# Two-layer graph kernel on one core: ScalarE normalises all rows of layer one's first eight blocks, the link factors are turned inside layer one, and layer two's first loads go out beside layer one's last stores

## What is computed

```python
edge_index = jnp.stack([src, dst])
h = jnp.maximum(_layernorm(x, axis=-1), 0.0)
# layer one: h @ W_self.T + b_self + segment_sum(h[col] @ W_neigh.T + b_neigh, row) / clip(count, 1)
x = x + _L0_gnn_ref(h, edge_index, L0_gnn_W_self, L0_gnn_b_self, L0_gnn_W_neigh, L0_gnn_b_neigh)
h = jnp.maximum(_layernorm(x, axis=-1), 0.0)
# layer two: relu(segment_sum(h[src] * norm[:, None], dst)), norm = deg[src] ** -0.5 * deg[dst] ** -0.5
x = x + _L1_gnn_ref(h, edge_index)
```

## Time and profile before

| | |
|---|---|
| median of 3 runs | 1185.05 us (1183.37 to 1186.17) |
| profiled execution, its own time | 1182.12 us |
| span of the profiled execution | 1180.3 us |
| busy: PE, DVE, ACT, POOL | 90%, 90%, 92%, 73% of the span |
| first gather of layer one, first gather of its last block | 27.8 us, 673.6 us |
| first row of layer two on ScalarE | 737.7 us |

### The profile page before, as it was taken

One profiled execution on the slowest core, in us unless ns is written; L12 is line 12 of the kernel. 1 busy time (PEld: TensorE's weight loads), 2 busy tenths in 40 slices (PEclk: granted clock), 3 DMA queues, 4 the chain that ended last, 5 costly groups with the idle time before them and its releaser, 6 DMA issues.

```text
span 1180.3 us, 30320 instructions
## 1 busy us (share of the span) xinstructions
PE 1057.1 (90%) x9408; PEld 955.5 (81%) x9408; DVE 1057.1 (90%) x3040; ACT 1082.5 (92%) x2871; POOL 862.4 (73%) x1143
## 2 busy tenths in 40 slices
PE   1388999999999999999999993799999999999998
PEld 1377999999989988989889992688888888888886
DVE  7779989989989989989989853899999999999995
ACT  2378999999989999999999991999999999999997
POOL 4767777777777877777777714888888888888870
PEclk9689999999999999999999997555555555555555
DMA  6325666767666766776667526499999999999994
GB/s 209 120 71 166 209 197 207 222 190 215 190 202 200 197 214 188 208 198 204 208 194 216 186 98 235 133 297 293 291 282 288 288 282 292 281 285 289 288 288 168
DMA packets 82232, 259.39 MB, mean 220 GB/s; under 512 B 19987, under 2 KB 20357, under 8 KB 82117
## 3 DMA queue, kind: packets, MB, share of 16 engines
q1 hardware_dynamic: 58948, 210.86, 57.3%
q0 software_dynamic: 22400, 46.91, 13.7%
q10 hardware_dynamic: 768, 0.20, 0.1%
HBM read 152.93 MB, written 104.37 MB: 218 GB/s over the span
## 4 chain that ended last, share of the span: by engine, by line
ACT 56%; POOL 15%; issue 11%; DVE 7%; PE 7%; DMA 3%; POOLq 0%; ACTq 0%; DVEq 0%
ACT work L739 24%; ACT p_O L739 14%; POOL X L634 12%; ACT p_T L739 6%; ACT area L754 4%; ACT p_c L739 3%; ACT area L749 2%; DMA X<-in_x,IDX 2%; DVE ST L1333 2%; PE p_O L910 2%; ACT sd L717 2%; POOL work L596 1%; PE p_O L922 1%; POOL work L592 1%; DVE p_O L1376 1%
## 5 line engine op out<-in xcount | busy, mean ns | idle before, releaser
L739 ACT ACTIVATE work<-X,shift,scale 128x128 f32<-128x128 f32 x1372 | 564.7, 512 | 1.8 <-DVE shift L1367 1.8
L634 POOL DMA_INDIRECT X<-in_x,IDX x392 | 387.4, 988 | 127.4 <-issue 98.6
L1333 DVE BATCH_NORM_STATS2 ST<-X 128x6 f32<-128x256 f32 x1176 | 408.2, 415 | 26.7 <-DMA X<-in_x,IDX 24.9
L968 PE MATMUL p_O<-work 32*128 32x128 f32 x1984 | 307.0, 436 | 44.4 <-DVE work L1350 24.8
L634 POOL DMA_INDIRECT X<-x_table,IDX x294 | 286.3, 974 | 76.5 <-issue 61.7
L968 PEld LDWEIGHTS p_O<-work 32*128 32x128 f32 x1984 | 263.9, 323 | 87.8 <-ACT work L739 31.1
L910 PE MATMUL p_O<-wnT,area 128*128 128x128 f32 x1568 | 218.0, 283 | 0.0
L922 PEld LDWEIGHTS p_O<-wsT,area 128*128 128x128 f32 x1568 | 207.2, 193 | 7.6
L922 PE MATMUL p_O<-wsT,area 128*128 128x128 f32 x1568 | 207.8, 276 | 0.0
L739 ACT ACTIVATE p_O<-X,shift,scale 128x128 f32<-128x128 f32 x496 | 199.1, 442 | 0.6 <-DVE shift L1367 0.6
L910 PEld LDWEIGHTS p_O<-wnT,area 128*128 128x128 f32 x1568 | 193.0, 194 | 0.3 <-DVE area L1386 0.3
(11 more groups left out here) (173 smaller groups left out, 1191.9 us busy)
## 6 DMA issues: line engine op xcount, KB each, us to landing
x_table<-area SPq DMA_DIRECT2D x98, 528.0 KB
X<-x_table SPq DMA_DIRECT2D x98, 528.0 KB
X<-in_x SPq DMA_DIRECT2D x98, 512.0 KB, 4.6
out_x<-area SPq DMA_DIRECT2D x98, 512.0 KB, 6.9
X<-in_x,IDX POOLq DMA_INDIRECT x392
X<-x_table,IDX POOLq DMA_INDIRECT x294
moved<-held SPq DMA_DIRECT2D x32, 12.2 KB
es<-in_src SPq DMA_DIRECT2D x1, 488.5 KB, 3.5
```

The lines of the kernel that those rows point to most:

```text
L634: nc.gpsimd.indirect_dma_start(got(s)[:, k, 0:w], None, table, bass.IndirectOffsetOnAxis(ap=IDX[:, s, k:k + 1], axis=0)).then_inc(gathered ...
L739: last = nc.scalar.activation(o, row(l, s, r), ACT.Relu, bias=shift[:, s, r:r + 1], scale=scale[:, s, r:r + 1])
L968: last = nc.tensor.matmul(outs1[p][g][:, P * col:P * col + P], SEL[1][q, p, part_of, :], H[1][q, p, draw, :], start=False, stop=(half == 1 ...
L1333: last = V.bn_stats(ST[:, s, r:r + 2, :].rearrange("p r k -> p (r k)"), pair.rearrange("p r c -> p c r"))
```

## The change

- **Rows.** For blocks 0 to 7 (`FIRST = 8`) ScalarE normalises all 12 rows; GpSimd's `last_row` begins with block 8.
- **Index lots.** `LOT[0]` is 2 where it was 5: GpSimd stages row numbers for two blocks at a time (49 copies for layer one where it had 20).
- **Start.** SyncE's first six loads wait until window 0 has arrived. VectorE's two digit cuts ahead of `marks(0)` now stand behind `double(0)`; the bias is split by GpSimd and ScalarE ahead of the windows; the work on group 1 moves from steps -4 to 3 to steps -1 to 6, `BEGIN` for group 2 from step 3 to 7. `START_AHEAD` grows over 15 blocks where it was 10.
- **Link factors.** They are transposed, two pieces in a step, in steps 82 to 85, and ScalarE copies them there (`take_dis`); SyncE spreads them in steps 86 to 89, VectorE adds two of them in step 93.
- **Layer two's first loads.** SyncE issues one of the eight behind each of layer one's last eight stores.

```diff
-LOT = (5, 4)
+LOT = (2, 4)
-START_AHEAD = (1, 1, 1, 1, 2, 2, 2, 3, 3, 3)
+START_AHEAD = (1,) * 4 + (2,) * 5 + (3,) * 6
+STARTING = 7
+FIRST = 8
-    BEGIN = {2: 3, 3: 17, 4: 31, 5: 45, 6: 58}
+    BEGIN = {2: 7, 3: 20, 4: 33, 5: 46, 6: 59}
+    TURN_AT, PASS_AT, DIS_AT = 82, 86, 93
+    def rows_of(i):
+        return range(0, ROWS if i < FIRST else ROWS - 1)
+    def dis_groups(k):
+        return [g for g in range(TB) if TURN_AT + g // 2 == k]
...
                 store(l, turn, old)
+                early = old + RING[0] - NB
+                if l == 0 and 0 <= early and old % RING[0] < RING[1]:
+                    b = old % RING[0]
+                    sp.wait_ge(stored[0][b % HR[0]], 16 * (b // HR[0] + 1))
+                    load(1, 0, b)
+            sp.wait_ge(s_win[0], 16)
             for s in range(EARLY):
                 load(0, 0, s)
...
             for s in range(EARLY, RING[0]):
+                sp.wait_ge(st_ready[0], s - EARLY + 2)
                 load(0, 0, s)
...
+                if k == PASS_AT:
+                    sp.wait_ge(s_disl, TB // 2 + 1)
+                    if PASS_AT + n // 4 == k:
+                        sp.dma_start(moved[to, 2, slot_of(of), :], DISL[of, j, :]).then_inc(s_moved, 16)
...
             def last_row(turn, off):
                 i, s, _ = place(0, turn, off)
+                if i < FIRST:
+                    return
...
+            def take_dis(k):
+                act.wait_ge(s_disT, dis_groups(k)[-1] // 2 + 1)
+                for g in dis_groups(k):
+                    c = slice(GROUP_BLOCKS * g, GROUP_BLOCKS * g + GROUP_BLOCKS)
+                    for a in range(2):
+                        q = slice(SLOTS * a, SLOTS * a + SLOTS)
+                        last = nc.scalar.copy(DISL[q, :, c].rearrange("p j n -> p n j"), ...)
+                last.then_inc(s_disl, 1)
...
                 if joins is not None:
                     turn_codes(joins)
+                for g in dis_groups(off):
+                    pe.wait_ge(s_dis2, 1)
+                    last = nc.tensor.transpose(turned_dis(g), dis2[:, g, :, :].rearrange("p a b -> p (a b)"), ident[0:TP, 0:TP])
+                    if g == dis_groups(off)[-1]:
+                        last.then_inc(s_disT, 1)
...
+                if dis_groups(off):
+                    pe.wait_ge(s_disl, dis_groups(off)[-1] // 2 + 1)
...
-                if off == NB:
-                    pe.wait_ge(s_dis2, 1)
-                    pe.wait_ge(prod_used[1], NB - 2)
-                    pe.wait_ge(sdeg_ready, NB)
-                    for b in range(TB):
...
+                if k == DIS_AT:
+                    dve.wait_ge(s_moved, 16 * 3 * 4 * PAIRS)
+                    V.tensor_tensor(moved[:, 2, 2, :], moved[:, 2, 2, :], moved[:, 2, 3, :], ALU.add).then_inc(s_tab1, 1)
...
             def fast():
-                act.wait_ge(s_disl, 1)
-                for to, of, j in moves():
-                    act.dma_start(moved[to, 2, slot_of(of), :], DISL[of, j, :]).then_inc(s_moved, 16)
                 schedule(1, act, step1)
...
             def fast():
-                dve.wait_ge(s_moved, 16 * 3 * 4 * PAIRS)
-                V.tensor_tensor(moved[:, 2, 2, :], moved[:, 2, 2, :], moved[:, 2, 3, :], ALU.add).then_inc(s_tab1, 1)
                 schedule(1, dve, step1)
```

More of the change, by code:

```diff
@@ L147, in joins_at @@
     def joins_at(k):
[L149 to L157, removed]
+        return 1 if k == 5 else next((g for g in BEGIN if BEGIN[g] + 11 == k), None)
+    def dis_groups(k):
+        return [g for g in range(TB) if TURN_AT + g // 2 == k]
     def either(eng, fast, general):
@@ L367, in gnn @@
         s_bias = sem("bias_placed")
+        s_bsum = sem("bias_rests_ready")
         s_tab = sem("group_tables_ready")
@@ L495, in general @@
             def general():
+                for s in range(RING[1]):
+                    sp.wait_ge(x_loaded[s], 16 * (len(range(s, NB, RING[0])) + 1))
                 sp.wait_ge(g_clean, 1)
@@ L543, in window @@
                     bass.IndirectOffsetOnAxis(ap=ptr_i[:, b:b + 1], axis=1)).then_inc(s_win[b], 16)
+            pool.wait_ge(s_w, 64)
+            nc.gpsimd.tensor_tensor(bsum[0:1, 0, :], brow[0:1, 0, :], brow[0:1, 1, :], ALU.add).then_inc(s_bsum, 1)
+            for k in range(2):
+                pool.wait_ge(s_bpart, k + 1)
+                nc.gpsimd.tensor_tensor(bsum[0:1, (k + 1) % 2, :], bsum[0:1, k % 2, :], bpart[0:1, k, 0, :], ALU.subtract
+                                        ).then_inc(s_bsum, 1)
             pool.wait_ge(s_ptr, 1)
@@ L572, in may_gather @@
                 i, s, _ = place(l, turn, off)
+                if l == 0 and i == EARLY:
+                    pool.wait_ge(s_found, 2)
+                    pool.wait_ge(s_facts, 4)
+                    pool.wait_ge(s_digits, 2 * len(CUTS))
+                    pool.sem_inc(idx_seen[0], 1)
                 if not first(i, RING[l]):
@@ L706, in _ @@
             nc.scalar.copy(wnT[:, :], p_O[2][:, D:2 * D]).then_inc(s_wcopied, 1)
-            digit(0)
-            digit(1)
+            for k in range(3):
+                act.wait_ge(s_bsum, k + 1)
+                nc.scalar.copy(bpart[0:1, k, :, :], bsum[0:1, k % 2, :].rearrange("p (j d) -> p j d", j=1
+                                                                                  ).to_broadcast([1, GT, D])).then_inc(s_bpart, 1)
             take_codes(0)
-            for n in range(2, 2 * len(CUTS)):
+            for n in range(2 * len(CUTS)):
                 digit(n)
@@ L785, in step0 @@
                 if there(0, turn, off + 1):
-                    normalise(0, turn, off + 1, range(MID, ROWS - 1))
+                    normalise(0, turn, off + 1, rows_of(off + 1)[MID:])
             def step1(turn, off):
@@ L794, in _ @@
             schedule(0, act, step0)
-            act.wait_ge(s_disT, 1)
-            for o, i in table_parts(DISL, banks_dis):
-                last = nc.scalar.copy(o, i)
-            last.then_inc(s_disl, 1)
             def fast():
-                act.wait_ge(s_disl, 1)
-                for to, of, j in moves():
-                    act.dma_start(moved[to, 2, slot_of(of), :], DISL[of, j, :]).then_inc(s_moved, 16)
                 schedule(1, act, step1)
@@ L1485, in then @@
                     dve.wait_ge(g_ord, order[0] if order[1] is None else order[1] + order[0])
+                for s in range(EARLY, RING[1]):
+                    dve.wait_ge(x_loaded[s], 16 * (len(range(s, NB, RING[0])) + 1))
                 dve.wait_ge(g_ord, 1)
```

93 lines of the change are left out of this document (39 added, 54 removed).

## The result

The changed kernel took 1189.54 us (median of 5, 1188.35 to 1191.19) where the kernel before took 1183.68 us (median of 5, 1182.39 to 1186.17): ratio 1.0047, interval 1.0033 to 1.006. It is half a per cent slower; the forecast of 1178 us and its range of 1170 to 1183.5 were wrong. The profiled execution took 1189.54 us (span 1187.7; before 1182.12 and 1180.3).

What follows compares the result with a forecast made beforehand. POOL, at 6.68 us a block, was taken to bound the end of layer one. Its terms gave +9.5 us, then -2.6, +0.7 and -0.5: 7.1 us faster, 1185.05 to 1178 us, range 1170 to 1183.5.

Steps and rivals of the forecast that it cites:

- (e): Layer one on POOL: 29 more index copies at 0.22 us each cost 6.4 us, lower bound 3.
- (c): Early blocks on POOL: no more waiting for group 1's row numbers, gain 4.7 us, bound 0.
- (a): Start of layer one: POOL's first gather comes 2.9 us earlier, as loads no longer share window 0's way.
- (d): POOL around block 13: new waits for TensorE from doubled statistics at steps 6 and 11, cost 3 us, bounds 0 and 8.
- (b): First eight blocks: POOL is spared eight last rows at 1.41 us each, gain 11.3 us.
- (g): Last stores of layer one: layer two's early loads delay the last store, cost 0.5 us, bounds 0 and 1.9.
- (f): End of layer one: link factors add 5.9 us on ACT and PE, 3.3 hidden, so cost 2.6.
- PE's tail: Seam: the link factors' transposes leave TensorE's tail, gain about 0.7 us.
- the prediction's own sign of being wrong: Early layer one: POOL waiting for DVE or PE before block 14 would show the forecast wrong; no size given.
- Slower: Rival, chance 0.08: each of the 29 index copies costs POOL 1.0 us, total 15 us slower, 1200 us.
- Start not won: Rival, chance 0.20: TensorE's half clock slows the first blocks, block 6 at 105 or later; gain 0 to 4 us.
- Larger gain: Rival, chance 0.17: no new waits, half-price copies, factor copies hidden in ACT's slack; gain 11 to 16 us.

Runs made afterwards that it cites:

- exp. 6: Kernel before with index lots of two in layer one (29 more copies), nothing else: 1192.11 us, ratio 1.0067.
- exp. 8: exp. 2 with POOL doing the last row of every block again (FIRST = 0): 1188.04 us, ratio 1.0036.
- exp. 2: Changed kernel with STARTING = 11, early loads behind all stores and link factors back at the seam: 1176.99 us, ratio 0.9923.
- exp. 3: Changed kernel with STARTING = 11 and link factors back at the seam, early loads kept: 1177.25 us, ratio 0.9948.
- exp. 1: Changed kernel with STARTING = 11 in place of 7, nothing else: 1181.63 us, ratio 0.9958.
- experiment 7: exp. 2 with index lots of two for the first 30 blocks only, then five: 1169.7 us, ratio 0.9883; 1450.18 us on a slow chip.
- experiment 4: Changed kernel with only the link factors back at the seam, STARTING left at 7: 1188.16 us, ratio 1.0034.
- experiment 5: Changed kernel with only layer two's first loads behind all stores; slow chips only: 1492.52 us (1.0229) and 1471.68 us (1.0269).
- experiment 9: experiment 7 with ScalarE taking the twelfth row for 16 blocks (FIRST = 16); slow chip only: 1481.23 us, ratio 1.0335.

## Why the prediction was wrong

Seven kernels, from the one before to the changed one, form a chain in which neighbours differ by one edit, or, in its second link, by all edits of the start. The differences of their ratios, at 1184 us, price each link. Such a difference is uncertain by 2 to 3 us (the intervals are 0.3% wide), so the differences of the medians (the kernel before at 1183.97) and of the start of layer two in the traces stand beside it; the chain closes by construction. Negative is slower.

| link | from, to (ratio) | by ratios | by medians | by traces | forecast |
|---|---|---|---|---|---|
| 29 copies (e), part of (c) | before, exp. 6: 1, 1.0067 | -7.9 | -8.1 | -9.9 | -6.4 |
| start (a), (d), rest of (c) | exp. 6, 8: 1.0067, 1.0036 | +3.7 | +4.1 | +4.2 | +4.6 |
| eight last rows (b) | exp. 8, 2: 1.0036, 0.9923 | +13.4 | +11.1 | +11.6 | +11.3 |
| early loads (g) | exp. 2, 3: 0.9923, 0.9948 | -3.0 | -0.3 | -1.7 | -0.5 |
| factors (f) and PE's tail | exp. 3, 1: 0.9948, 0.9958 | -1.2 | -4.4 | -4.9 | -1.9 |
| `STARTING` 11 to 7 | exp. 1, changed: 0.9958, 1.0047 | -10.5 | -7.9 | -6.6 | not in the sum |

The forecasts of the first two rows put all of (c) into the second, though the short lots of the first already end POOL's wait for group 1. Only the sum of both rows is a fair comparison: -4.2 us by the ratios for a forecast of -1.8.

**The step that failed is (d), the new waits.** It took -3 with a bound of -8, for VectorE's doubled statistics at steps 6 and 11. POOL waited 13.64 us before the last rows of blocks 9 to 13, which is the prediction's own sign of being wrong (POOL waiting for PE before block 14). Some 3 us of these are of the size that (d) gave: with the old order 3.32 are left. The other ten have another reason, `STARTING = 7`, a line in the diff to which the sum gave no term. I had read POOL's order around the first `last_row` and never followed ACT's and VectorE's order in steps 7 to 11, where the change moves a root ahead of a spill. Without it (experiment 1) the kernel is faster than the one before, with it slower, and both are clear of noise. At 1181.63 us experiment 1 is in the range, 3.6 above the forecast; the rest lies within the sizes of (e), (f) and (g), none of which is measured sharply.

`STARTING = 7` makes no instruction longer and adds none. ACT takes its instructions in order, so a wait ahead of the spill is one for TensorE, VectorE and POOL. The Trainium skill ("PSUM — Partial Sum Buffer", section "Engine vs sequencer instructions") says that the queues of ScalarE, VectorE and GpSimd are strictly first in, first out. The trace agrees for ScalarE: in step 8 TensorE's transposes for `spill_h` were done at 105.76 (the row L900 above), 2.99 us before the root in front of it began at 108.75, and the spill started only behind the root.

**(a) Earlier first gather: right, and for the reason given.** 27.77 to 24.74, 3.03 us for 2.9. From issue to landing, window 0 took 6.26 us before and 3.22 after the change:

```profile
7.92 6.26 DMA win<-in_pairs,ptr_i
```

```profile
8.00 3.22 DMA win<-in_pairs,ptr_i
```

**(b) Eight last rows: right in kind and size.** POOL's path sets the end of layer one; 11.1 us at block 92 and 11.05 us in the medians.

**(c) Group 1: right.** POOL did not wait before block 8, whose `last_row` began at 91.40 (forecast 94), 19.3 us earlier than before. "Step 6 ends at 90 to 94" was right too: `decode(1)` at its end was done on VectorE at 92.05, 0.6 us before POOL's copy for block 14 began at 92.65, and ACT's last row of that step ended at 94.27. That the wait is gone is the lots' doing and not the start's (experiment 6).

**(e) Copies: kind right, their own price right, the effect at the end perhaps larger.** In the changed kernel:

```profile
470.27 0.45 POOL L624 TENSOR_SCALAR work<-X,scale,shift 128x128 f32<-128x128 f32 x1
470.91 0.54 POOL L628 TENSOR_SCALAR work<-work 128x128 f32<-128x128 f32 x1 [0.20 <-POOL work L624]
471.41 0.18 POOL L592 COPY IDX<-SRC 128x8 int32<-128x8 int32 x1
472.09 1.05 POOL L666 DMA_INDIRECT X<-in_x,IDX  x1 [0.50 <-issue]
...
484.48 0.45 POOL L624 TENSOR_SCALAR work<-X,scale,shift 128x128 f32<-128x128 f32 x1
485.13 0.80 POOL L628 TENSOR_SCALAR work<-work 128x128 f32<-128x128 f32 x1 [0.20 <-POOL work L624]
485.89 0.18 POOL L592 COPY IDX<-SRC 128x8 int32<-128x8 int32 x1
486.31 1.05 POOL L666 DMA_INDIRECT X<-in_x,IDX  x1 [0.24 <-issue]
```

From a copy's start to the next gather it is 0.68 us in most of the 39 steady-state copies and 0.35 to 0.43 in six, but that gap says little: where it is short, L628 in front is longer. From the start of `last_row` to the next gather both kinds take 1.82 to 1.84 us in most blocks, and most blocks without a copy take 1.59 to 1.62. So a copy costs 0.22 us, as priced from the earlier trace rows, with 20 elements (kernel before) as with 8: the bound of -3 for smaller copies fell. The start-to-start of 1.0 us that *Slower* feared was seen in two of the 39. POOL's arrival at block 92 moved by more than 0.22 for each copy in experiments 6 and 7 (9.87 for 29, 7.01 for 20); what the rest is, or whether it is noise, isn't shown.

**(f) Factors: right within what can be measured.** On ACT steps 82 to 85 lost 4.2 us where 5.9 were forecast, 3.3 of them hidden. At the start of layer two the factors cost 2.4 us (experiment 4) and 1.3 (experiments 3 and 1), both counted from block 81, for a forecast of 1.9; the ratios give 1.5 and 1.2. The 11 to 12 us that ACT was to lie behind at block 92 were 12.18 (686.60 and 674.42).

**(g) Early loads: sign right, size short.** 1.0 to 1.8 us at the seam (experiment 3), for 0.5 with a bound of 1.9. "They take away loads that ran beside POOL's gathers" was right and gave nothing. The rule that I cited for (a) and against this term (in the Trainium skill's "DMA: Bandwidth & Descriptors", section "Issuing engines are not separate DMA queues", the DMAs of all issuing engines interleave on the same 16 engines) agrees with the trace in (a), where SyncE's loads and GpSimd's window are issued by different engines and the window took 6.26 us beside them and 3.22 without them. Here both loads and store are SyncE's, so the 4.37 to 4.80 us for 2.73 to 2.76 say nothing of different issuers.

**The rivals.** *Start not won* named the right place with a wrong cause: half clock as the brake, block 6 at 105 or later (98.08) and 1181 to 1185 us. The clock was 0.79 between 100 and 120 us, but was 1.00 without the waits, and the ring cost more than the case allowed. *Slower* came out in sign, by luck: its cause, copies at 1.0 us each and 1200 us, isn't what happened. *Larger gain* is what is left when the ring, the superfluous copies, the early loads and the factors' move are all undone (experiment 7, 1169.7 us).

## What to carry to other kernels

When a change shifts a threshold that decides an order, read the order on every engine around it, and ask of each instruction that waits what stands behind it: here a root ahead of a spill in five steps cost seven to ten microseconds and turned the gain into a loss. A lead (how many blocks ahead a result is made) and the place of its consumer in the step belong together; move one only with the other. Price a small repeated instruction from a fixed row ahead of it to the next row behind it, with and without it, over all occurrences: the gap behind it alone was 0.68 or 0.42 us here for the same cost of 0.22. And compare two traces from a point where they should still agree: here identical code was 3.6 us apart.

## What the runs showed of the hardware

The same kernel can take up to 23% longer, far more than these kernels differ. On two of the five chips that the experiments ran on, the kernel before took 1460.8 us (1459.19 to 1462.18, 15 runs) and 1431.7 us (1426.81 to 1437.45, 17 runs); on the other three it took 1183.82 to 1186.3. Each chip was used once, so whether it is the chip or the moment isn't shown. The loss is spread over the whole program: experiment 6's kernel has ACT busy 415.04 us of 500 (200 to 700 us) on such a chip and 480.50 on an ordinary one. There the five kernels that start layer one early and give ScalarE the twelfth rows (experiments 1, 4, 5, 7 and 9) also stood still near its beginning, for 48.7 to 49.0 us. Experiment 7 on such a chip, ACT's timeline and, below it, two stretches:

```profile
87.35 1.07 ACT L794 COPY area<-p_T 128x512 f32<-128x512 f32 x2 [48.70 <-remote]
```

```profile
40.00:60.00 20.00, 1.48 (x7) 0.98 (x7) 0.00 (x0) 0.00 (x0) 15.52 (x18) 0.56 0.25 73
60.00:80.00 20.00, 0.00 (x0) 0.00 (x0) 0.00 (x0) 0.00 (x0) 15.57 (x18) 0.50 0.20 52
```

ACT stood for 48.70 us with a releaser that the profile calls "remote", PE, DVE and ACT did nothing between 60 and 80 us, and POOL went on with its gathers. On an ordinary chip the same kernel's root of block 0 came at 46.92 us in place of 95.83. Experiment 8, where ACT waits for POOL's twelfth row in the first blocks, had it at 67.53 there and at 58.50 on an ordinary chip. What holds the engines there isn't settled: the trace names no instruction for it. The practical side: a difference of a per cent between kernels on such a chip (1.0136 for the kernel that is 0.9883 on an ordinary one) says nothing about the other chips.
